# Attention scores packed into full banks, and one-hot tiles made by another engine

## The chip, the core and the metric

The kernel runs on one core of a Trainium2 chip. A core has five engines that run their own instruction streams and meet at semaphores: TensorE (PE in the profile; its weight loads are PEld), VectorE (DVE), ScalarE (ACT), GpSimd (POOL) and SyncE (SP), which here only issues DMAs. The metric is the time of one execution on the device in microseconds; several executions are timed and the median is taken.

## What is computed

Two layers, each an attention followed by a mixture of experts, on 8 batches of 512 tokens with 256 features. Cut to what matters here:

```python
x = x + tanh(g_xattn[0]) * L0_xattn(layernorm(x), ctx, ctx)   # 16 heads of 16, causal softmax
x = x + tanh(g_ffn[0])   * L0_ffn(layernorm(x))               # 32 experts, top 8, capacity 256
x = x + tanh(g_xattn[1]) * L1_xattn(layernorm(x), ctx, ctx)   # no causal mask
x = x + tanh(g_ffn[1])   * L1_ffn(layernorm(x))               # 8 experts, top 2
```

The first experts need, for each of their 32 * 256 = 8192 slots, the token that was routed there.

## The kernel before

Four phases run one after the other: `attention` for layer 0, `experts0`, `attention` for layer 1, `experts1`. The change lies in the first.

**The iterations.** `attention` works on one batch per iteration and has several batches in flight. Iteration `it` computes the scores of batch `cur = it`, the row maxima of batch `nxt = it + 1`, projections of later batches (`nn`, `n3`), and finishes earlier ones: `prev = it - 1` gets its output projection, second norm and routing, and `done = it - 2` gets its entries in the slot table. Iterations run from -3 to 9. Each is 64 steps `u`, and every engine's stream is written out by hand in the order of these steps; no scheduler changes it. An engine that has to wait holds back all that stands behind it in its stream.

**Scores, exponentials, values.** Heads come in four groups `g` of four. For a group, PE computes transposed scores, key tile `kt` (128 keys) against queries. With the causal mask only queries from `128 * kt` on are needed, so the four key tiles have 512, 384, 256 and 128 columns. `scores(b, u)` does one head and key tile per step: a matmul (L699), a second one (L702) that adds the mask to the diagonal 128 columns, into one of three PSUM banks `stb` of 512 columns. ACT's `exps` (L741) turns the bank into weights `pt`, which signals `st_free`. Then `values` (L713) multiplies the weights of one key tile of four heads by the values `va`, four matmuls into the four 32-row quarters of the bank `ob`. It is called once per key tile, at steps 6, 10, 14 and 18 after the group's start. After the fourth call ACT copies `ob` out (`outputs`, L746).

**Maxima.** The row maxima of `nxt` (PE L686 and L689, DVE L873 and L869) go through two banks `mxb`, at the steps 0, 2, 3, 5 and 7 of every eight.

**The other work of PE** stands in the table `TRIPS`: step, kind, batch. `x` at 24 and 31 transposes the normalised input of `n3`, `list` at 18, 20, 25 and 28 is the slot table, `p` the output projection, and so on. They share two banks `work`.

**The slot table.** For batch `done`, DVE makes four pairs of tiles (`one_hot`): `lo1` (128 tokens x 8 x 128, a one where the slot's low part is) and `hv` (x 8 x 64, the token's number where its high part is). DVE does so at 16 steps of the iteration, two instructions for `lo1` (L1021), one compare (L1024) and one multiplication (L1028) for `hv`. Each pair signals `lo_rdy` to the `list` matmuls (L665), and two pairs of buffers alternate. After the fourth `list`, DVE's `enlist` adds the result up (L1035 to L1039) at step 29 and frees the bank, which `x` at step 31 takes next.

**GpSimd** has little to do in this phase: the third parts of a three-way split of queries and keys (`rest` L1123, `low` L1129, at steps 61, 5, 16, 22) and the reciprocal roots of the two norms (`norm1` L1110 to L1117 at step 14, `norm2` L1134 to L1138 at step 29). ACT applies the first norm at steps 16, 17, 18 and 20 (L787, which signals `xn_rdy`), works on the split at 3 and 21 (L807), and applies the second norm at 33 to 36 (L798).

Of the kernel before, what the change touches and what calls it, by code (L numbers as in the profile page):

```python
# [248 lines left out]
def attention(c, layer, x_in, ctx_in, mask, wq, bq, wk, bk, wv, bv, wp, bp, wroute, x_out, rows,
# [17 lines left out]
    MAX_NO = {u: i for i, u in enumerate(sorted(MAX_BANKS))}  # L267

    with ExitStack() as ctx:
# [22 lines left out]
        pt = t_("pt", [P, 8, S])  # L292
# [292 lines left out]
        def _(pe):  # L585
# [119 lines left out]
            def values(b, g, kt):  # L705
                if g == 0 and kt == 0:
                    pe.wait_ge(evac["v"], 2 * b + 2)
                pe.wait_ge(s["st_free"], STEPS * b + 16 * g + 4 * kt + 4)
                if kt == 0:
                    wait(pe, s["ob_evac"], 4 * b + g)  # L710
                q0 = q_from(kt)
                for j in range(4):
                    last = pe.matmul(ob[32 * j:32 * j + 32, q0:S], va[b % 3][:, kt, 4 * g + j, :],  # L713
                                     pt[:, 4 * (kt % 2) + j, q0:S], start=kt == 0, stop=kt == NT - 1,
                                     tile_position=(0, 32 * j))
# [19 lines left out]
        def _(act):  # L735
            def exps(b, u):
                kt = u % 16 // 4
                if u % 4 == 0:
                    wait(act, s["pt_free"], 16 * b + u // 4 - 1)
                act.wait_ge(s["st_full"], STEPS * b + u + 1)  # L740
                act.activation(pt[:, u % 8, q_from(kt):S], stb[(STEPS * b + u) % N_ST][:, q_from(kt):S], ACT.Exp, scale=SCALE).then_inc(s["st_free"], 1)  # L741

            def outputs(b, g):
                act.wait_ge(s["pt_free"], 16 * b + 4 * g + 4)
# [892 lines left out]
```

## Time and profile before

| | us |
|---|---|
| median of three executions | 2114.45 (2112.62 to 2115.19) |
| the profiled execution, its own time | 2112.23 |
| its span, first to last instruction | 2110.4 |

The span divides into stages; the first `attention` takes the first five:

| us from the span's start | what runs |
|---|---|
| 0 to 120.4 | constants, weights, iterations -3 to -1 |
| 120.4 to 306.7 | iterations 0 to 2 (slot table from iteration 2 on) |
| 306.7 to 505 | iterations 3 to 5 (the first two of them full, with all kinds of work) |
| 505 to 608 | iterations 6 and 7, with no batch left to prepare |
| 608 to 655 | iterations 8 and 9: routing and slot table of the last two batches |
| 655 to 2110 | `experts0`, the second attention, `experts1` |

Reading the rows: a timeline row gives start, duration, engine, line, operation, output and inputs, the count of merged instructions, and in brackets the idle time before it with what ended it. A PE row's duration includes time in which the next matmul already runs, so PE's pace is read from the distance between starts.

### The profile page before, as it was taken

To read this page: it belongs to the slowest core of one execution; us is meant where nothing else is said; L and a number is where in the kernel's file an instruction comes from. 1 tells how busy PE (TensorE), PEld (TensorE's weight loads), DVE (VectorE), ACT (ScalarE), POOL (GpSimd) and SP (SyncE) were. 2 spreads that over 40 slices of the span, in tenths; PEclk is the share of its full clock that TensorE was granted. 3 is DMA by queue.
4 is the path that set the end of the run, shared out by engine and by line. 5 is a ranking of instruction groups with operands and counts; after the bars stand their busy time and mean duration, and the time that the engine had idled before them with its cause. 6 is when DMAs were issued, how large, how long until landed. Compare 5 with 4: busy or idle time off the path is not lost. (4 is left out here: it accounts for less than half of the span.)

```text
span 2110.4 us, 30079 instructions
## 1 busy us (share of the span) xinstructions
PE 1790.4 (85%) x10491; PEld 1054.6 (50%) x10491; DVE 1063.8 (50%) x2743; ACT 908.0 (43%) x1876; POOL 598.3 (28%) x577
## 2 busy tenths in 40 slices
PE   2789999999865999537899999999954999999995
PEld 1445555555534877413344444443331666666664
DVE  3446777887745444244867777778420211212121
ACT  1356766666541222113577777776730111111110
POOL 1312111210002778503211332221122233333322
PEclk9999999999986999858999999999976999999998
DMA  3444554434123788525323433331014133333314
GB/s 96 152 120 150 150 176 134 132 129 141 65 83 99 175 173 173 91 66 159 108 72 116 136 97 95 120 117 62 32 47 136 31 81 81 78 78 75 80 20 100
DMA packets 204245, 222.86 MB, mean 106 GB/s; under 512 B 33438, under 2 KB 195231, under 8 KB 203431
## 3 DMA queue, kind: packets, MB, share of 16 engines
q1 hardware_dynamic: 176458, 177.48, 27.4%
q0 software_dynamic: 27648, 43.60, 10.9%
q8 instruction: 78, 1.28, 0.3%
q14 instruction: 61, 0.50, 0.1%
HBM read 155.06 MB, written 86.93 MB: 115 GB/s over the span
## 5 line engine op out<-in xcount | busy, mean ns | idle before, releaser
L873 DVE TENSOR_REDUCE nmx<-mxb 128x1 f32<-128x512 f32 (+1 forms) x896 | 522.7, 609 | 282.5 <-PE mxb L686 146.6
L741 ACT ACTIVATE pt<-stb 128x512 f32<-128x512 f32 (+3 forms) x1024 | 501.0, 519 | 266.3 <-PE stb L702 140.8
L686 PE MATMUL mxb<-kst,qst 96*128 96x512 bf16 (+4 forms) x1024 | 332.3, 346 | 30.2 <-DVE nmx L873 21.3
L699 PE MATMUL stb<-qst,kst 99*128 99x512 bf16 (+4 forms) x1024 | 342.4, 345 | 14.8 <-DMA qst<-m3T 8.4
L713 PE MATMUL ob<-pt,va 128*32 128x512 f32 (+3 forms) x2048 | 233.7, 528 | 3.8 <-ACT oT L746 2.8
L1428 PE MATMUL e_h_bank<-e_xT,e_w 128*128 128x512 f32 x512 | 226.0, 600 | 6.1 <-ACT e_xT L1468 5.4
L699 PEld LDWEIGHTS stb<-qst,kst 102*128 102x128 bf16 (+1 forms) x1024 | 100.1, 99 | 258.1 <-ACT pt L741 167.3
L1442 PE MATMUL e_y_bank<-e_w,e_h 128*128 128x256 f32 x1024 | 226.9, 379 | 0.0
L1442 PEld LDWEIGHTS e_y_bank<-e_w,e_h 128*128 128x128 f32 x1024 | 192.9, 190 | 31.8 <-issue 7.2
L1123 POOL TENSOR_TENSOR qk<-qk,parts 128x512 f32<-128x512 f32 x64 | 72.8, 1160 | 432.8 <-ACT qk L774 225.7
L1582 POOL DMA_INDIRECT x_after_l<-e_y,e_token x64 | 99.6, 1556 | 281.7 <-DVE e_y L1547 267.0
L686 PEld LDWEIGHTS mxb<-kst,qst 99*128 99x128 bf16 (+1 forms) x1024 | 100.7, 99 | 133.9 <-DVE nmx L873 72.4
L1428 PEld LDWEIGHTS e_h_bank<-e_xT,e_w 128*128 128x128 f32 x512 | 97.8, 192 | 125.6 <-issue 125.0
L1477 ACT ACTIVATE e_h<-e_h_bank,e_b_e 128x512 f32<-128x512 f32 x64 | 44.0, 687 | 270.6 <-PE e_h_bank L1428 270.6
L1532 DVE TENSOR_SCALAR e_h<-e_h_bank,e_b_e 128x512 f32<-128x512 f32 x64 | 48.0, 750 | 171.5 <-PE e_h_bank L1428 171.5
L1543 DVE TENSOR_TENSOR e_y<-e_y_bank,e_b 128x512 f32<-128x512 f32 x32 | 22.1, 691 | 201.6 <-PE e_y_bank L1442 201.6
L1335 POOL DMA_INDIRECT x_after_l<-e_y,token x64 | 102.2, 1598 | 44.4 <-issue 17.6
L702 PE MATMUL stb<-hide_st,identb 128*128 128x128 bf16 x512 | 110.6, 221 | 0.0
L689 PE MATMUL mxb<-hide_max,identb 128*128 128x128 bf16 x512 | 110.0, 221 | 0.0
L1129 POOL TENSOR_TENSOR parts<-qk,parts 128x512 bf16<-128x512 f32 x64 | 73.9, 1175 | 97.8 <-ACT parts L807 97.8
L1144 POOL DMA_INDIRECT rows<-rowb,idx x64 | 63.9, 998 | 114.5 <-DVE idx L1000 97.4
L1243 PE MATMUL e_bank<-e_xT,e_guT 128*128 128x256 f32 x384 | 88.6, 380 | 1.0 <-DVE e_h L1299 1.0
(231 smaller groups left out, 2493.1 us busy)
## 6 DMA issues: line engine op xcount, KB each, us to landing
qk_parts<-parts SPq DMA_DIRECT2D x16, 1536.0 KB, 6.2
qst<-qk_parts SPq DMA_DIRECT2D x384, 64.0 KB, 2.3
kst<-qk_parts SPq DMA_DIRECT2D x384, 64.0 KB, 2.3
e_w<-in_L_ffn_w SPq DMA_DIRECT2D x16, 1024.0 KB, 7.4
rows<-rows SPq DMA_DIRECT2D x15, 1060.0 KB, 8.6
crow<-in_ctx SPq DMA_DIRECT2D x16, 512.0 KB, 3.9
x_after_l<-xres SPq DMA_DIRECT2D x16, 512.0 KB, 3.2
e_gu_nat<-in_L_ffn_gate_up_proj SPq DMA_DIRECT2D x64, 128.0 KB
```

Source lines behind the costliest of these rows:

```text
L686: last = pe.matmul(out, qst[par][0:rows_used, h, qt * P:(qt + 1) * P], kst[par][0:rows_used, h, 0:nk], start=True, stop=not causal)
L689: last = pe.matmul(out[:, nk - P:nk], c.identb[:, :], c.hide_max[:, :], start=False, stop=True)
L699: last = pe.matmul(out[:, q0:S], kst[par][0:ROWS, h, kt * P:(kt + 1) * P], qst[par][0:ROWS, h, q0:S], start=True, stop=not causal)
L702: last = pe.matmul(out[:, q0:q0 + P], c.identb[:, :], c.hide_st[:, :], start=False, stop=True)
L713: last = pe.matmul(ob[32 * j:32 * j + 32, q0:S], va[b % 3][:, kt, 4 * g + j, :], pt[:, 4 * (kt % 2) + j, q0:S], start=kt == 0, stop=kt == ...
L741: act.activation(pt[:, u % 8, q_from(kt):S], stb[(STEPS * b + u) % N_ST][:, q_from(kt):S], ACT.Exp, scale=SCALE).then_inc(s["st_free"], 1)
L873: last = dve.tensor_reduce(nmx[:, qt, h:h + 1], got[:, at:at + k_to(qt)], AX.X, ALU.max, negate=True)
L1243: last = pe.matmul(out, guT[par][:, ci, q, :], xT[par][:, ci, :], start=ci == 0, stop=ci == NC - 1)
L1335: pool.indirect_dma_start(x, bass.IndirectOffsetOnAxis(token[:, TILES * e + i:TILES * e + i + 1], 0), y[e % 3][:, i, :], None, bounds_chec ...
L1428: last = pe.matmul(hb[q % 4][:, :], w1_s[par][:, ci, k * P:(k + 1) * P], xT[par][:, ci, blk * HALF:(blk + 1) * HALF], start=ci == 0, stop= ...
L1442: last = pe.matmul(yb[t][:, i * D:(i + 1) * D], h[blk][:, k, (2 * t + i) * P:(2 * t + i + 1) * P], w2_s[par][:, k, :], start=k == 0, stop= ...
L1582: pool.indirect_dma_start(x, bass.IndirectOffsetOnAxis(token[par][:, i:i + 1], 0), y[par][:, i, :], None, bounds_check=T + SPARE - 1, oob_ ...
```

## The change

Scores of the first attention are packed so that every bank is full: a bank holds key tile 0 of one head, or tiles 3 and 1 of one head (128 + 384 columns), or tile 2 of two heads (256 + 256). A group has 10 banks in place of 16, at the steps 0, 2, 3, 5, 7, 8, 10, 11, 13, 15, and an exponential always takes 512 columns. `values` is called twice per group, at step 10 for key tile 0 and at step 18 for tiles 1, 3 and 2. The weights `pt` have 10 slots, one per bank of a group, in place of 8. For batches 0 to 6 GpSimd makes the one-hot tiles, 16 small instructions per pair, at the steps 6, 10, 13 and 19 of its stream; DVE makes those of batch 7 as before. There are three pairs of buffers. The second attention keeps one head and key tile per bank and four calls per group.

```diff
--- before.py
+++ after.py
@@ -226,6 +226,7 @@
+N_HOT = 3
...
+def score_banks(packed):
+    banks = {}
+    for g in range(GROUPS):
+        if not packed:
+            banks.update({16 * g + u: ((4 * g + u % 4, u // 4, 0),) for u in range(16)})
+            continue
+        for j, u in enumerate((0, 2, 3, 5)):
+            banks[16 * g + u] = ((4 * g + j, 0, 0),)
+        for j, u in enumerate((7, 8, 10, 11)):
+            banks[16 * g + u] = ((4 * g + j, 3, 0), (4 * g + j, 1, P))
+        for j, u in enumerate((13, 15)):
+            banks[16 * g + u] = ((4 * g + 2 * j, 2, 0), (4 * g + 2 * j + 1, 2, 2 * P))
     return banks
...
+    PACKED = causal
+    SCORE_BANKS = score_banks(PACKED)
+    N_SCORE = len(SCORE_BANKS)
+    SCORE_NO = {u: i for i, u in enumerate(sorted(SCORE_BANKS))}
+    VALUE_CALLS = {10: (0,), 18: (1, 3, 2)} if PACKED else {6: (0,), 10: (1,), 14: (2,), 18: (3,)}
+    N_CALL = len(VALUE_CALLS) * GROUPS
...
+    PT_SLOTS = 10 if PACKED else 8
...
-            lo1 = [t_(f"lo1_{i}", [P, 8, P], BF16) for i in range(2)]
-            hv = [t_(f"hv{i}", [P, 8, N_HI], BF16) for i in range(2)]
+            lo1 = [t_(f"lo1_{i}", [P, 8, P], BF16) for i in range(N_HOT)]
+            hv = [t_(f"hv{i}", [P, 8, N_HI], BF16) for i in range(N_HOT)]
...
-                wait(sp, s["st_full"], STEPS * (n - 2) + 16 * g + 16)
+                wait(sp, s["st_full"], N_SCORE * (n - 2) + N_SCORE // GROUPS * (g + 1))
...
             def scores(b, u):
...
-                wait(pe, s["st_free"], STEPS * b + u - N_ST + 1)
-                q0, h = q_from(kt), 4 * g + j
-                out = stb[(STEPS * b + u) % N_ST]
-                last = pe.matmul(out[:, q0:S], kst[par][0:ROWS, h, kt * P:(kt + 1) * P],
-                                 qst[par][0:ROWS, h, q0:S], start=True, stop=not causal)
-                if causal:
-                    last = pe.matmul(out[:, q0:q0 + P], c.identb[:, :], c.hide_st[:, :], start=False, stop=True)
+                if u not in SCORE_BANKS:
+                    return
+                no = N_SCORE * b + SCORE_NO[u]
+                wait(pe, s["st_free"], no - N_ST + 1)
+                bank = stb[no % N_ST]
+                for h, kt, at in SCORE_BANKS[u]:
+                    to = at if PACKED else q_from(kt)
+                    last = pe.matmul(bank[:, to:to + S - q_from(kt)], kst[par][0:ROWS, h, kt * P:(kt + 1) * P],
+                                     qst[par][0:ROWS, h, q_from(kt):S], start=True, stop=not causal)
+                    if causal:
+                        last = pe.matmul(bank[:, to:to + P], c.identb[:, :], c.hide_st[:, :], start=False, stop=True)
                 last.then_inc(s["st_full"], 1)
...
-                    if u == 2 and prev is not None:
-                        values(prev, 3, 3)
-                    if u % 4 == 2 and u > 2 and cur is not None:
-                        values(cur, (u - 6) // 16, (u - 6) % 16 // 4)
+                    for call, at in enumerate(sorted(VALUE_CALLS)):
+                        if u == at - 16 and prev is not None:
+                            values(prev, GROUPS - 1, call)
+                        if u >= at and (u - at) % 16 == 0 and cur is not None:
+                            values(cur, (u - at) // 16, call)
...
-                kt = u % 16 // 4
-                if u % 4 == 0:
-                    wait(act, s["pt_free"], 16 * b + u // 4 - 1)
-                act.wait_ge(s["st_full"], STEPS * b + u + 1)
-                act.activation(pt[:, u % 8, q_from(kt):S], stb[(STEPS * b + u) % N_ST][:, q_from(kt):S], ACT.Exp, scale=SCALE).then_inc(s["st_free"], 1)
...
+                if PACKED and u % 16 in (0, 7):
+                    wait(act, s["pt_free"], N_CALL * b + u // 16 * 2 - (1 if u % 16 == 0 else 0))
...
+                act.activation(pt[:, slot(b, u), q0:S], stb[no % N_ST][:, q0:S], ACT.Exp, scale=SCALE).then_inc(s["st_free"], 1)
...
+                    wait(dve, s["lo_rdy"], 4 * b)
...
-                        if u in ONE_HOT_AT:
+                        if u in ONE_HOT_AT and done == B - 1:
                             one_hot(done, ONE_HOT_AT.index(u) // 4, ONE_HOT_AT.index(u) % 4)
...
+            def one_hot(b, t):
+                pool.wait_ge(s["idx_rdy"], b + 1)
+                wait(pool, full["list"], 4 * b + t - N_HOT + 1)
+                for k in range(8):
+                    pool.tensor_scalar(lo1[t % N_HOT][:, k, :], c.lanes[:, :], lo_f[:, t, k:k + 1], None, ALU.is_equal)
+                for k in range(8):
+                    last = pool.tensor_scalar(hv[t % N_HOT][:, k, :], c.lanes[:, 0:N_HI], hi_f[:, t, k:k + 1], c.tok1[:, 0:1], ALU.is_equal, ALU.mult)
+                last.then_inc(s["lo_rdy"], 1)
...
+                    if layer == 0 and done is not None and done < B - 1 and u in (6, 10, 13, 19):
+                        one_hot(done, (6, 10, 13, 19).index(u))
```

PE, steps 18 and 19 of a full iteration, the start of a group's second half of `values`. Before, with the key tile 3 alone (L713) ahead of the first `list`:

```order
L686 MATMUL mxb_0<-kst_0,qst_0 128x512 [waits max_free_0]
L689 MATMUL mxb_0<-hide_max,identb 128x128
L713 MATMUL ob<-pt,va_0 32x128 [waits st_free_0]
L713 MATMUL ob<-pt,va_0 32x128 x3
L665 MATMUL work_0<-hv_0,lo_0_0 128x64 [waits lo_rdy_0,p_evac_0]
```

The same place after, where L757 is `values` and L703 `list`:

```order
L724 MATMUL mxb_0<-kst_0,qst_0 128x512 [waits max_free_0]
L727 MATMUL mxb_0<-hide_max,identb 128x128
L757 MATMUL ob<-pt,va_0 32x384 [waits st_free_0]
L757 MATMUL ob<-pt,va_0 32x384 x3
L757 MATMUL ob<-pt,va_0 32x128 x4
L757 MATMUL ob<-pt,va_0 32x256 x4
L703 MATMUL work_0<-hv_0,lo_0_0 128x64 [waits lo_rdy_0,p_evac_0]
```

Three key tiles now follow each other with one wait ahead of them.

GpSimd, one full iteration from `low` of the queries (step 5) to the second norm (step 29). Before:

```order
L1129 TENSOR_TENSOR parts<-qk,parts 128x512 x2
L1110 TENSOR_SCALAR rstd<-mv 128x4
L1112 TENSOR_TENSOR rstd<-rstd,mhalf 128x4
L1117 TENSOR_TENSOR shift_0<-minus_0,rstd 128x4
L1123 TENSOR_TENSOR qk<-qk,parts 128x512 x2
L1129 TENSOR_TENSOR parts<-qk,parts 128x512 x2
L1134 TENSOR_SCALAR rstdb<-mvb 128x4
```

After, with the same operations at L1181, L1162 to L1169, L1175 and L1186:

```order
L1181 TENSOR_TENSOR parts<-qk,parts 128x512 x2
L1203 TENSOR_SCALAR lo_0_0<-lanes,lo_f 128x128 x8
L1205 TENSOR_SCALAR hv_0<-lanes,hi_f,tok 128x64 x8
L1203 TENSOR_SCALAR lo_1_0<-lanes,lo_f 128x128 x8
L1205 TENSOR_SCALAR hv_0<-lanes,hi_f,tok 128x64 x8
L1203 TENSOR_SCALAR lo_2_0<-lanes,lo_f 128x128 x8
L1205 TENSOR_SCALAR hv_0<-lanes,hi_f,tok 128x64 x8
L1162 TENSOR_SCALAR rstd<-mv 128x4
L1164 TENSOR_TENSOR rstd<-rstd,mhalf 128x4
L1169 TENSOR_TENSOR shift_0<-minus_0,rstd 128x4
L1175 TENSOR_TENSOR qk<-qk,parts 128x512 x2
L1203 TENSOR_SCALAR lo_0_0<-lanes,lo_f 128x128 x8
```

Three tile pairs now stand ahead of the first norm and of the keys' `rest`, and the fourth ahead of the keys' `low`.

## Rows read from the trace of the kernel before

**Rows 1.** Busy time by stretch: length, busy time and count per engine, PE clock, DMA

```profile
306.70:505.00 198.30, 186.97 (x1659) 112.77 (x1658) 154.72 (x440) 127.77 (x298) 35.38 (x39) 1.00 0.45 139
...
608.00:655.00 47.00, 19.25 (x142) 14.52 (x142) 28.32 (x85) 5.37 (x10) 1.47 (x3) 0.61 0.14 48
```

**Rows 2.** Timeline of PE in the full iteration that starts at 306.7

```profile
313.30 0.22 PE L702 MATMUL stb<-hide_st,identb 128*128 128x128 bf16 x1
313.45 1.06 PE L713 MATMUL ob<-pt,va 128*32 128x512 f32 x8
314.45 0.34 PE L699 MATMUL stb<-qst,kst 102*128 102x384 bf16 x1
314.62 0.22 PE L702 MATMUL stb<-hide_st,identb 128*128 128x128 bf16 x1
314.68 0.38 PE L686 MATMUL mxb<-kst,qst 99*128 99x512 bf16 x1
...
326.04 0.22 PE L689 MATMUL mxb<-hide_max,identb 128*128 128x128 bf16 x1
326.19 0.43 PE L713 MATMUL ob<-pt,va 128*32 128x128 f32 x8
326.54 0.41 PE L665 MATMUL work<-hv,lo 128*128 128x64 bf16 x8
```

**Rows 3.** PE's waits in iterations 2 to 4: us in total, times, longest

```profile
PE work L665 <- DVE hv L1028: 4.0, 3, 1.3
PE work L607 <- DVE listed L1036: 3.3, 3, 1.2
```

**Rows 4.** PE's waits for DVE's maxima in iteration 6

```profile
PE mxb L686 <- DVE nmx L873: 2.1, 4, 1.1
```

**Rows 5.** PE's waits for ACT in iteration 0, then in iteration 7

```profile
PE stb L699 <- ACT pt L741: 1.2, 3, 0.6
...
PE stb L699 <- ACT pt L741: 3.0, 3, 2.2
```

**Rows 6.** Groups of GpSimd by form, whole span: busy us, mean ns, idle before

```profile
L1123 POOL TENSOR_TENSOR qk<-qk,parts 128x512 f32<-128x512 f32 x64 | 72.8, 1160 | 432.8 <-ACT qk L774 225.7 <-ACT qk L778 207.0
...
L1110 POOL TENSOR_SCALAR rstd<-mv 128x4 f32<-128x4 f32 x16 | 3.8, 234 | 162.4 <-DVE minus L861 162.4
...
L196 POOL TENSOR_SCALAR_AFFINE_SELECT identb<-identb 128x128 bf16<-128x128 bf16 x1 | 0.3, 293 | 0.0
...
L190 POOL MEMSET identb<- 128x128 bf16 x1 | 0.2, 218 | 0.0
```

**Rows 7.** Timeline of GpSimd in the same full iteration

```profile
311.66 2.58 POOL L1129 TENSOR_TENSOR parts<-qk,parts 128x512 bf16<-128x512 f32 x2 [2.91 <-ACT parts L807]
322.94 0.25 POOL L1110 TENSOR_SCALAR rstd<-mv 128x4 f32<-128x4 f32 x1 [8.70 <-DVE minus L861]
...
331.39 2.28 POOL L1129 TENSOR_TENSOR parts<-qk,parts 128x512 bf16<-128x512 f32 x2 [4.57 <-ACT parts L807]
```

**Rows 8.** Timeline of ACT, same iteration: first norm applied, first and last part

```profile
324.65 0.59 ACT L787 ACTIVATE xn<-xin,shift,rstd 128x256 f32<-128x256 f32 x1
...
329.30 0.59 ACT L787 ACTIVATE xn<-xin,shift,rstd 128x256 f32<-128x256 f32 x1
```

**Rows 9.** Timeline of PE, same iteration: first `x` and fourth `list`

```profile
332.81 0.60 PE L607 MATMUL work<-ident,xn 128*128 128x128 f32 x4
...
337.64 0.41 PE L665 MATMUL work<-hv,lo 128*128 128x64 bf16 x8 [1.32 <-DVE hv L1028]
```

**Rows 10.** Groups of ACT by form in the same full iteration

```profile
L741 ACT ACTIVATE pt<-stb 128x512 f32<-128x512 f32 x16 | 9.2, 595 | 3.0 <-PE stb L702 3.0
...
L741 ACT ACTIVATE pt<-stb 128x128 f32<-128x128 f32 x18 | 4.5, 282 | 6.4 <-PE stb L702 6.3
```

**Rows 11.** A group of DVE by form in the same full iteration

```profile
L1021 DVE TENSOR_TENSOR lo<-lanes,lo_f 128x512 bf16<-128x512 bf16 x8 | 5.8, 733 | 0.0
```

**Rows 12.** Timeline of PE in iteration 8: the fourth `list`

```profile
625.36 0.61 PE L665 MATMUL work<-hv,lo 128*128 128x64 bf16 x8 [3.12 <-DVE hv L1028]
```

More of the change, by code:

```diff
@@ L245, in shared_banks @@
         banks[u + 7] = ((h + 1, 3, 0),)
+    return banks
+def score_banks(packed):
[10 more added lines that the diff above has]
+            banks[16 * g + u] = ((4 * g + 2 * j, 2, 0), (4 * g + 2 * j + 1, 2, 2 * P))
     return banks
@@ L291, in attention @@
         va = [t_(f"va{i}", [P, NT, HEADS, 32]) for i in range(3)]
-        pt = t_("pt", [P, 8, S])
+        pt = t_("pt", [P, PT_SLOTS, S])
         oT = [t_(f"oT{i}", [P, S]) for i in range(2)]
@@ L496, in k_to, with quad, slot, weights_of @@
             return (qt + 1) * P if causal else S
+        def quad(b, u):
+            return (STEPS * b + u) // 4
+        def slot(b, u):
+            if PACKED:
+                return SCORE_NO[u] % (N_SCORE // GROUPS)
+            return quad(b, u) % (PT_SLOTS // 4) * 4 + u % 4
+        def weights_of(b, g, kt, j):
+            if not PACKED:
+                return pt[:, slot(b, 16 * g + 4 * kt + j), q_from(kt):S]
+            at, first = {0: (0, j), 1: (P, 4 + j), 2: (2 * P * (j % 2), 8 + j // 2), 3: (0, 4 + j)}[kt]
+            return pt[:, first, at:at + S - q_from(kt)]
         @block.sync
@@ L664, in trip @@
                     for k in range(8):
-                        done = pe.matmul(out[:, N_HI * part:N_HI * (part + 1)], lo1[part % 2][:, k, :], hv[part % 2][:, k, :],
+                        done = pe.matmul(out[:, N_HI * part:N_HI * (part + 1)], lo1[part % N_HOT][:, k, :], hv[part % N_HOT][:, k, :],
                                          start=k == 0, stop=k == 7)
@@ L703, in scores, with values @@
                 last.then_inc(s["st_full"], 1)
-            def values(b, g, kt):
-                if g == 0 and kt == 0:
+            def values(b, g, call):
+                at = sorted(VALUE_CALLS)[call]
+                if g == 0 and call == 0:
                     pe.wait_ge(evac["v"], 2 * b + 2)
-                pe.wait_ge(s["st_free"], STEPS * b + 16 * g + 4 * kt + 4)
-                if kt == 0:
+                scored = sum(u < 16 * (g + 1) and u // 16 == g and {kt for _, kt, _ in SCORE_BANKS[u]} <= USED[at] for u in SCORE_BANKS)
+                pe.wait_ge(s["st_free"], N_SCORE * b + N_SCORE // GROUPS * g + scored)
+                if call == 0:
@@ L710, in values @@
                     wait(pe, s["ob_evac"], 4 * b + g)
[L711 to L715, printed above, removed]
+                for kt in VALUE_CALLS[at]:
+                    for j in range(4):
+                        last = pe.matmul(ob[32 * j:32 * j + 32, q_from(kt):S], va[b % 3][:, kt, 4 * g + j, :],
+                                         weights_of(b, g, kt, j), start=kt == 0, stop=kt == VALUE_CALLS[max(VALUE_CALLS)][-1],
+                                         tile_position=(0, 32 * j))
@@ L736, in exps @@
             def exps(b, u):
[L737 to L741 removed]
+                if u not in SCORE_BANKS:
+                    return
+                no = N_SCORE * b + SCORE_NO[u]
+                if PACKED and u % 16 in (0, 7):
+                    wait(act, s["pt_free"], N_CALL * b + u // 16 * 2 - (1 if u % 16 == 0 else 0))
+                if not PACKED and u % 4 == 0:
+                    last = quad(b, u) - PT_SLOTS // 4
+                    wait(act, s["pt_free"], last // (4 // len(VALUE_CALLS)) + 1)
+                act.wait_ge(s["st_full"], no + 1)
+                q0 = 0 if PACKED else q_from(SCORE_BANKS[u][0][1])
+                act.activation(pt[:, slot(b, u), q0:S], stb[no % N_ST][:, q0:S], ACT.Exp, scale=SCALE).then_inc(s["st_free"], 1)
             def outputs(b, g):
[L744 removed]
+                act.wait_ge(s["pt_free"], N_CALL * b + len(VALUE_CALLS) * (g + 1))
                 wait(act, full["o"], 4 * b + g - 1)
```

15 lines of the change are left out of this document (8 added, 7 removed).

## The prediction

> **What bounds the kernel now.** I read the stretches first [rows 1]. In iterations 3 to 5 PE is busy 187.0 of 198.3 us; DVE has 154.7, ACT 127.8, GpSimd 35.4. So the first attention goes at PE's pace, and work that leaves DVE or ACT counts only where PE waits for it. A PE that is busy in this sense could still stand behind late starts, so next I read the distance between its starts [rows 2]: 512 columns of `values` take 1.00 us, 384 columns of scores 0.17, a mask 0.06. These repeat to the hundredth, so PE runs full, at the granted clock of 1.00 (2.4 GHz), except where a wait shows. In the full iterations 2 to 4 the waits are two: the fourth `list` waits for DVE's one-hot tile, 1.32 us each time, and `x` at step 31 waits for `enlist`, 1.1 on average [rows 3]. In the thinner iteration 6 PE also waits 2.1 us for maxima of a DVE that has fallen behind [rows 4]; in iteration 7 it waits 3.0 us for ACT, and 1.2 in iteration 0 [rows 5]. In 608 to 655 nothing bounds but the chain of one batch's steps; PE is busy 19.3 of 47 us at a clock of 0.61 [rows 1].
>
> **The change part by part.**
>
> *Values in two calls.* A mask is followed by the next bf16 matmul after 0.06 us, but by `values` after 0.15: 0.09 for the turn to the four-quarter form. And the call with 128 columns takes 0.35, with 512 columns 1.00 [rows 2]; a straight line through them gives 0.217 per 128 columns and a rest of 0.13 that doesn't grow with the columns. Merging three calls into one saves two turns per group: 2 x 4 groups x 8 batches = 64. Each saves 0.09 if blocks inside a call still pay the rest, 0.22 if they don't: 5.8 to 14.1 us. All of it is on PE's path. I take the middle, 0.16 x 64 = **10 us**.
> The Trainium skill, TensorEngine Tiling (Array Packing), Key Properties, says that changing the tiling mode drains the engine while changing the tile alone doesn't. The 0.09 agrees; if the rest of 0.13 is the drain as well, the saving is the 14.1, and the sum below would be 4 us lower.
>
> *Exponentials.* 64 become 40 per batch, with the same columns: 16 x (0.595 + 0.282) plus the middle sizes become 40 x 0.595 = 23.8 us [rows 10]; a 512 costs far less than four times a 128. ACT isn't the bound, so this gives only PE's waits for ACT back. Three banks now hold about 4.8 steps of work in place of 3, so iteration 0's waits go: **1 us** of 1.2 [rows 5].
>
> *Scores.* The same 64 + 64 matmuls per batch with the same columns: nothing. They now come only at steps that also carry maxima, so PE reaches the next maxima sooner at some steps and later at others. In the full iterations no wait for maxima is among PE's long ones, and where DVE was loaded with tiles and PE had less to do it came to 2.1 us [rows 4]. I take 0, and up to that 2.1 per batch as the other end.
>
> *One-hot tiles off DVE.* DVE loses the 5.8 us of L1021 per iteration [rows 11] and the two smaller groups that make `hv`. *They land on GpSimd*, which has no row for such an instruction. Below, a 128-column AFFINE_SELECT, one input and one output of just this shape, takes 0.29 us; a memset 0.22. A TENSOR_SCALAR of 4 columns takes 0.23, and the slope of a two-input TENSOR_TENSOR, (1.160 - 0.23) / 508, is 1.83 ns per column [rows 6]. So a 128-column one costs 0.25 to 0.46 and a 64-column one 0.15 to 0.34, a pair of tiles (8 of each) 3.2 to 6.4 us. Nearest is the AFFINE_SELECT, with a little for the scalar read per partition: 0.32 and 0.24, **4.5 us per pair**. That is 18 us per iteration on an engine that is mostly idle, but in a fixed order.
>
> What stands behind it: `low` ends at 314.24, +7.5 after the iteration's start at 306.7 [rows 7]; with `values` now 1.7 us long at step 2, ACT gets to its part later, so +8.4. Three pairs follow. Then `norm1`, which now starts at 322.94 after 8.7 us of idle, +16.2 [rows 7]. Then ACT's four norm instructions with two exponentials and a copy between them; they now run from 324.65 to 329.89 [rows 8], and without waits for PE would take about 3.6. `x` on PE at step 24 needs them. So `x` can start at 8.4 + 3t + 1.6 + 3.6 = 13.6 + 3t, where t is the time per pair; PE comes to it at +26.1 now [rows 9], +25.5 after. At t = 3.9 PE begins to wait; at 4.5 it waits 1.6 us. The fourth pair comes after `norm1` and `rest` (3.7 with the start at 8.4): ready at 12.1 + 4t, against +29.0 for the fourth `list` (now 337.64 less the wait of 1.32 and the merged calls [rows 9]). At 4.5 that is +30.1, covered by the wait at `x`. So in iterations 2 to 4 a wait of 1.6 replaces one of 1.32: **+1 us** in all, where t = 3.2 gives -4 and t = 6.4 gives +17 (7.3 against 1.32). The wait for `enlist` stays almost whole: after the fourth `list` DVE must take the maxima of step 29 and then add up, with `x` two steps behind. I leave 0.9 of the 1.1: **-0.5** for the three.
> GpSimd's `low` of the keys, now at 331.39, shifts by about 2.7 us at t = 4.5, and SP's store of the parts with it; the stacked rows it feeds are needed an iteration later, so this is hidden.
>
> *Thin iterations.* 5 has no `norm1`, so the fourth pair is ready at 10.5 + 4t = +28.5: a tile wait like those of rows 3 goes, 1.3, and I add as much for DVE's lag behind it: **-2.5**. 6 has no split on GpSimd; the tile wait of 1.3 and the 2.1 of maxima go [rows 3, 4]: **-3.5**. In 7, 3.0 us of waits for ACT [rows 5] come from the second norm, which stands behind `enlist`; the tiles end at 1 + 4t = +19 of about +20: **-2.5**.
>
> *Tail.* In iteration 8 the fourth `list` runs at 625.36 [rows 12]. On GpSimd the four pairs start near 608 and end near 626: **+1**, and the last call of `values` is 1.3 longer with nothing beside it, partly paid back in iteration 7: **+1**. At t = 3.2 this is -1, at 6.4 +9.
>
> *Sum.* -10 - 1 + 1 - 0.5 - 2.5 - 3.5 - 2.5 + 2 = **-17**. The profiled execution took 2112.2, so 2095; the median of the runs stands 2.2 above it, so a median of runs may come out up to 2 higher. I say **2096**.
>
> **Rivals.**
> *GpSimd is dear (slower).* If a compare costs what the two-input rows say, t = 6.4: iterations 2 to 4 lose 17, iteration 5 loses 6 (10.5 + 4t is then 36 against 29, less the 1.3), 7 loses 5, the tail 9, against 10 of calls, 2 in iteration 6 and 1.5 of the rest: +23, 2137 with the median's 2. It decides from t = 5.4, where losses and gains are even; at t = 6 it is about 2130. For it: no row shows the operation, and a scalar per partition is an extra operand. Against: AFFINE_SELECT's 0.29.
> The Trainium skill, GPSIMD Engine Reference, Engine selection, speaks against the change: elementwise work belongs on VectorE, though it calls one-input work roughly line-rate, which would be this forecast's side. No row here settles it.
> *GpSimd is cheap and merged blocks flow.* t = 3.2 and 14.1 us of calls: -14 - 1 - 4 - 1 - 3 - 4 - 4 - 1 = -32, 2080.
> *The gains are given back (no change).* Bursts of banks make PE wait for DVE's maxima, 2.1 us per batch as in rows 4, in 8 batches: -17 + 17, so 2112 to 2114. For it: banks and maxima now share their steps. Against: DVE has at least 5.8 us less to do per iteration [rows 11].
>
> **How the numbers follow.** Forecast 0.50 (2084 to 2108), cheap 0.20, given back 0.14, dear 0.16. Two of ten outside means cutting the lower half of the cheap case and the upper half of the dear one: 2076 to 2120. About 0.2%, 4 us, is what can be told from no change: faster 0.72, same 0.12, slower 0.16.
>
> **What would show it.** Right: GpSimd rows of 128 columns near 0.32 us and of 64 near 0.24; two turns fewer per group, with the long call near 1.6 us between starts; no PE wait for DVE's `hv`, but one of 1 to 2 us at `x` of step 24 put down to ACT's `xn`, behind GpSimd; the `listed` wait still there; iteration 6 at least 3.5 us shorter. Wrong: compare rows over 0.4 us, `list` waiting for GpSimd, ACT idle behind `norm1`, or full iterations that stay at 66 us with waits for maxima.

## The result, and the profile after

The changed kernel takes 2228.74 us (median of 2227.05 to 2235.4) against 2114.82 for the kernel before in the same comparison: a ratio of 1.0543, 95% interval 1.0527 to 1.0559. It is slower by 114 us; the forecast was 2096, and the range ended at 2120. The profiled execution took 2227.05 us, with a span of 2225.3.

First the operation that no row of before showed. Groups of GpSimd by line: operation, output and input, count, then busy us and mean ns.

```profile
L1203 POOL TENSOR_SCALAR lo<-lanes,lo_f 128x128 bf16<-128x128 bf16 x224 | 131.1, 630 | 74.0 <-DVE hi_f L1062 74.0
L1205 POOL TENSOR_SCALAR hv<-lanes,hi_f,tok 128x64 bf16<-128x64 bf16 x224 | 126.0, 616 | 0.0
```

The forecast took 0.32 and 0.24 us; they are 0.63 and 0.62. The records overlap a little: from start to start, in the rows below, it is 0.58 and 0.55, and eight of each make 9.1. Next GpSimd's timeline in the full iteration 3, which answers to [rows 7]: start, duration, what ran; in brackets the idle time ahead.

```profile
321.79 2.32 POOL L1175 TENSOR_TENSOR qk<-qk,parts 128x512 f32<-128x512 f32 x2 [30.52 <-ACT qk L829]
328.89 2.27 POOL L1181 TENSOR_TENSOR parts<-qk,parts 128x512 bf16<-128x512 f32 x2 [4.78 <-ACT parts L858]
331.14 4.67 POOL L1203 TENSOR_SCALAR lo<-lanes,lo_f 128x128 bf16<-128x128 bf16 x8
335.80 4.48 POOL L1205 TENSOR_SCALAR hv<-lanes,hi_f,tok 128x64 bf16<-128x64 bf16 x8
...
358.34 0.30 POOL L1162 TENSOR_SCALAR rstd<-mv 128x4 f32<-128x4 f32 x1
...
362.24 4.68 POOL L1203 TENSOR_SCALAR lo<-lanes,lo_f 128x128 bf16<-128x128 bf16 x8
366.90 4.48 POOL L1205 TENSOR_SCALAR hv<-lanes,hi_f,tok 128x64 bf16<-128x64 bf16 x8
371.32 2.29 POOL L1181 TENSOR_TENSOR parts<-qk,parts 128x512 bf16<-128x512 f32 x2
```

From 331.14 to 371.32 GpSimd has no idle time. A pair follows the last after 9.1 us (331.14 to 340.23), and `norm1` starts at 358.34, 36.6 us after GpSimd's first row of the iteration, where it had come 16.2 into the iteration [rows 7]. Who waits for this is in PE's waits, 120 to 780 us (total, times, longest):

```profile
PE work L703 <- POOL hv L1205: 75.4, 18, 8.5
PE stb L741 <- ACT pt L792: 27.7, 4, 10.2
PE work L703 <- DVE hv L1080: 10.2, 4, 5.6
```

The third row belongs to batch 7, whose tiles DVE still makes; `listed` is left with 1.2 us. The second row is ACT behind the late `norm1`: its norm instructions stand ahead of exponentials in its stream, and PE then finds no free `stb` bank. The prediction had put this wait at `x` of step 24; PE meets it earlier, at the scores. In order of time, those of PE's rows from 340 to 377 us (iteration 3) that have a wait:

```profile
349.42 0.61 PE L703 MATMUL work<-hv,lo 128*128 128x64 bf16 x8 [3.41 <-POOL hv L1205]
...
361.70 0.29 PE L741 MATMUL stb<-qst,kst 102*128 102x128 bf16 x1 [8.76 <-ACT pt L792]
...
371.43 0.41 PE L703 MATMUL work<-hv,lo 128*128 128x64 bf16 x8 [2.65 <-POOL hv L1205]
...
374.03 1.11 PE L645 MATMUL work<-ident,xn 128*128 128x128 f32 x4 [0.89 <-DVE listed L1088]
```

These four give 15.7 us, and the iteration is 20.3 longer. The rest shows in the whole iteration 3, after and then before: length, busy time and count of PE, PEld, DVE, ACT and POOL, PE's clock, DMA.

```profile
323.06:409.92 86.86, 68.14 (x557) 42.50 (x555) 44.64 (x132) 41.16 (x79) 48.34 (x79) 0.88 0.41 124
306.53:373.05 66.52, 63.11 (x556) 38.10 (x554) 51.77 (x148) 43.78 (x103) 12.34 (x15) 1.00 0.48 148
```

All of PE's waits in it are 18.9 us against 3.4, so 15.5 more, and PE is busy 5.0 us longer with as many matmuls: between and after long waits its granted clock falls. PE by stretches of 20 us: length, busy time and count, clock, DMA:

```profile
320.00:340.00 20.00, 18.07 (x147) 1.00 0.67 196
340.00:360.00 20.00, 9.54 (x80) 0.81 0.00 1
360.00:380.00 20.00, 14.75 (x100) 0.67 0.33 105
380.00:400.00 20.00, 19.20 (x189) 1.00 0.51 148
```

Before, the mean over iterations 3 to 5 was 1.00, 2.4 GHz [rows 1]; 0.67 and 0.81 are means between that and 1.2 GHz. In the stretch of 0.81 PE waits 3.4 us for GpSimd and most of the 8.8 for ACT behind it.

DVE's cast of the slot numbers runs once per iteration, at its start (L1009 before, L1061 after); counted from it, this is where the fourth `list` stands and how long the iteration is:

| iteration | fourth `list`, before | after | later by | length before | after | longer by |
|---|---|---|---|---|---|---|
| 2 | 31.1 | 48.4 | 17.3 | 66.2 | 84.8 | 18.7 |
| 3 | 31.1 | 48.4 | 17.3 | 66.5 | 86.9 | 20.3 |
| 4 | 31.1 | 48.4 | 17.3 | 66.5 | 86.6 | 20.1 |
| 5 | 30.9 | 46.8 | 15.8 | 64.2 | 82.1 | 17.9 |
| 6 | 26.6 | 36.8 | 10.2 | 59.0 | 68.6 | 9.5 |
| 7 | 19.9 | 36.8 | 16.9 | 44.5 | 58.8 | 14.3 |
| 8 | 18.2 | 36.8 | 18.6 | 37.3 | 56.0 | 18.6 |
| sum | | | 113.4 | | | 119.4 |

Outside these iterations the span is 4.5 us shorter, 2.1 of it ahead of iteration 2. So the loss goes with the lateness of the fourth `list`, to about 3 us in each iteration, and nothing of the packing's gain shows but a little in iterations without tiles.

### The profile page after: what moved, and what is told of

It is laid out like the page before. It is cut to its first block and busy times, and to the rows that moved or that the text cites. A ratio compares the mean times of both kernels' runs of the same rounds, so it can differ in the third digit from the quotient of the medians.

```text
span 2225.3 us, 30165 instructions
## 1 busy us (share of the span) xinstructions
PE 1805.7 (81%) x10491; PEld 1076.4 (48%) x10491; DVE 1010.3 (45%) x2631; ACT 886.9 (40%) x1684; POOL 851.0 (38%) x1025
## 5 line engine op out<-in xcount | busy, mean ns | idle before, releaser
L792 ACT ACTIVATE pt<-stb 128x512 f32<-128x512 f32 x832 | 475.1, 598 | 323.8 <-PE stb L744 199.9
L724 PE MATMUL mxb<-kst,qst 96*128 96x512 bf16 (+4 forms) x1024 | 340.5, 354 | 34.4 <-DVE nmx L924 25.0
L741 PE MATMUL stb<-qst,kst 99*128 99x512 bf16 (+4 forms) x1024 | 336.9, 354 | 37.4 <-ACT pt L792 29.7
L1175 POOL TENSOR_TENSOR qk<-qk,parts 128x512 f32<-128x512 f32 x64 | 73.0, 1165 | 426.4 <-ACT qk L825 223.3
L757 PE MATMUL ob<-pt,va 128*32 128x512 f32 (+3 forms) x2048 | 224.2, 533 | 2.7 <-ACT pt L792 1.7
L1203 POOL TENSOR_SCALAR lo<-lanes,lo_f 128x128 bf16<-128x128 bf16 x224 | 131.1, 630 | 74.0 <-DVE hi_f L1062 74.0
L1205 POOL TENSOR_SCALAR hv<-lanes,hi_f,tok 128x64 bf16<-128x64 bf16 x224 | 126.0, 616 | 0.0
L744 PE MATMUL stb<-hide_st,identb 128*128 128x128 bf16 x512 | 115.6, 232 | 0.0
```

The lines of the kernel that those rows point to most:

```text
L724: last = pe.matmul(out, qst[par][0:rows_used, h, qt * P:(qt + 1) * P], kst[par][0:rows_used, h, 0:nk], start=True, stop=not causal)
L741: last = pe.matmul(bank[:, to:to + S - q_from(kt)], kst[par][0:ROWS, h, kt * P:(kt + 1) * P], qst[par][0:ROWS, h, q_from(kt):S], start=Tru ...
L744: last = pe.matmul(bank[:, to:to + P], c.identb[:, :], c.hide_st[:, :], start=False, stop=True)
L757: last = pe.matmul(ob[32 * j:32 * j + 32, q_from(kt):S], va[b % 3][:, kt, 4 * g + j, :], weights_of(b, g, kt, j), start=kt == 0, stop=kt = ...
L792: act.activation(pt[:, slot(b, u), q0:S], stb[no % N_ST][:, q0:S], ACT.Exp, scale=SCALE).then_inc(s["st_free"], 1)
L1203: pool.tensor_scalar(lo1[t % N_HOT][:, k, :], c.lanes[:, :], lo_f[:, t, k:k + 1], None, ALU.is_equal)
```

## The experiments

**Packing alone.** All tiles back on DVE; the third pair of buffers stays:

```diff
-                        if u in ONE_HOT_AT and done == B - 1:
+                        if u in ONE_HOT_AT:
```

> Packed scores and two calls of values as in the changed kernel, with all one-hot tiles left on DVE. Theory 1 (GpSimd's tiles cost about 9.1 us a pair and all that stands behind them, packing itself gains): 2100 to 2107 us, 8 to 15 below the 2115 of before, with the 64 merged calls worth 6 to 14. Rival (packing itself costs time, because banks and maxima share their steps): above 2117, with PE waits for DVE's maxima of over 2 us per batch.

Measured: 2119.52, ratio 1.0023 (1.0012 to 1.0034). Packing is slower by itself: the rival's time, though its waits for maxima are 1.2 us and not over 2. PE's waits in iteration 3, against 1.3 for `hv`, 1.2 for `listed`, 0.7 for DVE's sequencer (DVEq) and 0.2 for `m3T` before. `nmx` are the row maxima, `xres` the residual sum, `listed` the slot table's sum; `onT` and `m3T` are copies that ACT makes of a PE result for a later matmul:

```profile
PE work L645 <- DVE listed L1088: 1.6, 1, 1.6
PE mxb L724 <- DVE nmx L924: 1.2, 1, 1.2
PE work L645 <- DVE xres L957: 1.0, 1, 1.0
PE work L703 <- DVE hv L1080: 0.8, 1, 0.8
PE work L676 <- ACT onT L810: 0.7, 1, 0.7
PE work L665 <- ACT m3T L864: 0.6, 1, 0.6
```

With two smaller ones these are 6.4 us against 3.4, and the iteration is 68.2 long against 66.5: the work between waits shrank by about 1.4 us (PE is busy 61.7 against 63.1), and the new waits took 3.0. The merged call itself does what it should:

```profile
326.44 1.50 PE L757 MATMUL ob<-pt,va 128*32 128x384 f32 x24
327.87 0.41 PE L703 MATMUL work<-hv,lo 128*128 128x64 bf16 x8
```

The three tiles have 768 columns, 1.30 us at the 0.217 per 128 of the prediction; the block takes 1.43. So the rest of 0.13 is paid once per call.

**Tiles on GpSimd alone.** The scores unpacked:

```diff
-    PACKED = causal
+    PACKED = False
```

> One-hot tiles on GpSimd as in the changed kernel, scores and values unpacked as before. Theory 1: 2230 to 2245 us, since the whole loss comes from GpSimd and packing only gave some of it back. Rival (packing costs a large part of the 114): 2140 to 2200.

Measured: 2219.48, ratio 1.0499 (1.0484 to 1.0515), below the first theory's range and above the rival's. The tiles account for 105 of the 114 us, and packing comes on top with 9 (2228.7 against 2219.5), where it was to take 11 away. In iteration 3 (82.1 us long, against 86.9 with packing) PE waits 16.9 us, 15.3 of them at once for ACT behind `norm1`, and is busy 65.2. So of the 4.8 that packing adds there, 2.0 are more waits and 2.9 a longer busy PE, whose mean clock is 0.88 against 0.90.

**Half the tiles.** GpSimd makes `lo`, DVE makes `hv` (scores packed):

```diff
-                for k in range(8):
-                    last = pool.tensor_scalar(hv[t % N_HOT][:, k, :], c.lanes[:, 0:N_HI], hi_f[:, t, k:k + 1], c.tok1[:, 0:1], ALU.is_equal, ALU.mult)
```

> As the changed kernel, but GpSimd makes only the lo1 tiles (8 instructions, about 4.7 us a pair) and DVE the hv tiles. This gives the chain on GpSimd nearly the 4.5 us per pair that the prediction assumed. If only the size of that term was wrong and the rest of the sum holds: 2095 to 2106 us, with a wait of 1 to 3 us at x of step 24 and none for GpSimd's tiles in the full iterations. Rival (other terms fail too, for example because a waiting PE loses its clock, or because two engines must finish each pair): 2110 to 2150.

Measured: 2113.93, ratio 0.9998 (0.9988 to 1.0008). Eight `lo` instructions took 4.96 us here, near the 4.5 that the forecast had put on a whole pair, and the loss is gone. But nothing is gained: the time lies in the rival's range and not in the 2095 to 2106 of a sum in which only this size was wrong, so other terms failed too. In the full iterations PE waits for ACT, 4.1 us in six waits, none over 1.2, and once 0.3 for `lo`. In iteration 3 the two for ACT are 1.4, and 0.2 more for `xn`: the 1.6 behind `norm1` that the prediction worked out for such a dose. The waits that packing alone makes for `nmx`, `onT` and `m3T` stand beside them, a full iteration takes 68.1 to 69.1 us, and in the thinner ones PE waits 9.2 for `lo`. So the chain on GpSimd behaves as worked out once its price is put in; what packing was to gain is missing here as well.

**The forms.** In the constants of the kernel before, GpSimd runs four instructions of each of nine forms:

```diff
+                pool.tensor_scalar(bdst[:, 0 + k, :], bsrc[:, 0:P], scal[:, k:k + 1], None, ALU.is_equal)
+                pool.tensor_scalar(bdst[:, 4 + k, :], bsrc[:, 0:P], 1.0, None, ALU.is_equal)
+                pool.tensor_scalar(bdst[:, 8 + k, 0:4], bsrc[:, 0:4], scal[:, k:k + 1], None, ALU.is_equal)
+                pool.tensor_scalar(bwide[:, 512 * k:512 * k + 512], bsrc[:, :], scal[:, k:k + 1], None, ALU.is_equal)
...
+                pool.tensor_scalar(fdst[:, 20 + k, :], fsrc[:, 0:P], scal[:, k:k + 1], None, ALU.mult)
...
+                pool.tensor_scalar(bdst[:, 28 + k, 0:64], bsrc[:, 0:64], scal[:, k:k + 1], scal[:, 0:1], ALU.is_equal, ALU.mult)
+                pool.tensor_scalar(bdst[:, 32 + k, 0:64], bsrc[:, 0:64], scal[:, k:k + 1], None, ALU.is_equal)
```

> The kernel before with nine groups of four TENSOR_SCALAR instructions of GpSimd added to the constants, to price the form (in order: compare bf16 128 columns with a scalar per partition; the same with a constant; 4 columns with a scalar per partition; 512 columns; f32 compare 128; f32 multiply 128; bf16 multiply 128; compare and multiply bf16 64 columns; compare bf16 64). Theory A (the scalar per partition costs a fixed 0.4 us): constant form under 0.35 us, 4 columns at 0.45 or more, 512 columns about 0.9. Theory B (the compare is slow per column): 4 columns near 0.25, 512 columns near 1.6, multiply near 0.35. Theory C (bf16 is slow): the f32 forms near 0.35.

```profile
L221 POOL TENSOR_SCALAR bwide<-bsrc,scal 128x512 bf16<-128x512 bf16 x4 | 6.2, 1566 | 0.0
...
L215 POOL TENSOR_SCALAR bdst<-bsrc,scal 128x128 bf16<-128x128 bf16 x4 | 2.4, 610 | 0.1
L225 POOL TENSOR_SCALAR fdst<-fsrc,scal 128x128 f32<-128x128 f32 x4 | 2.4, 605 | 0.0
...
L229 POOL TENSOR_SCALAR bdst<-bsrc,scal 128x64 bf16<-128x64 bf16 x4 | 2.2, 576 | 0.0
L217 POOL TENSOR_SCALAR bdst<-bsrc 128x128 bf16<-128x128 bf16 x4 | 2.0, 526 | 0.1
L231 POOL TENSOR_SCALAR bdst<-bsrc,scal 128x64 bf16<-128x64 bf16 x4 | 1.7, 438 | 0.0
L219 POOL TENSOR_SCALAR bdst<-bsrc,scal 128x4 bf16<-128x4 bf16 x4 | 1.1, 294 | 0.0
```

From 4 to 512 columns the slope is (1566 - 294) / 508 = 2.5 ns per column. Type and operation change nothing (bf16 compare 610, fp32 multiplication 605), a constant in place of the scalar per partition saves 84 ns, and the second operation of `hv` costs 138 on 64 columns. None of the theories holds whole. What was missed is plain: one input, but a steeper slope than two. The prediction's 1.83 joined a TENSOR_SCALAR to a TENSOR_TENSOR [rows 6]; from TENSOR_TENSOR's own rows before, 4 columns in 0.20 us (L1117) and 512 in 1.16, it is 1.89. Of `hv`'s price the second operation is 0.14, for which the forecast had nothing.

**A dose below the slack.** Scores as before the change; of four pairs GpSimd makes the last alone, in the third pair of buffers, `lo` ahead of its own `low` and `hv` behind it:

```diff
-                        if u in ONE_HOT_AT and done == B - 1:
+                        if u in ONE_HOT_AT and (done == B - 1 or ONE_HOT_AT.index(u) < 12):
...
-                    if layer == 0 and done is not None and done < B - 1 and u in (6, 10, 13, 19):
+                    if layer == 0 and done is not None and done < B - 1 and u in (4, 6):
```

> The kernel before in its scores, exponentials and calls of values; of the four tile pairs of a batch GpSimd makes only the last (its lo part ahead of its own low of the queries, its hv part behind it), DVE the other three. Theory 'a dose below the slack': two times 4.6 us per iteration end about 7 us before the fourth list needs them, and norm1 starts at most 1 us later; DVE loses a quarter of its tile work, so the 1.3 us wait for DVE's hv in iterations 2 to 4 goes and the lag in 5 to 7 shrinks: 2104 to 2110. Rival 'GpSimd slows DVE': DVE's two-input compares of the other pairs take 0.2 us longer each while GpSimd works, as the hv compare did with the lo tiles on GpSimd (0.99 against 0.81 us), and little is left: 2111 to 2116. Rival 'slow tiles cost something anywhere': a quarter of the loss of after, some 2135.

Measured: 2102.27, ratio 0.9932 (0.9918 to 0.9946). The first theory holds, a little beyond its range. PE's wait for `hv` in iterations 2 to 4 [rows 3] is gone and that for `listed` shrinks to 0.7 at most; a full iteration takes 64.4 us against 66.5. GpSimd pays for working beside DVE's tiles:

```profile
L1209 POOL TENSOR_SCALAR lo<-lanes,lo_f 128x128 bf16<-128x128 bf16 x48 | 36.0, 765 | 55.6 <-DVE hi_f L1066 55.6
L1213 POOL TENSOR_SCALAR hv<-lanes,hi_f,tok 128x64 bf16<-128x64 bf16 x48 | 31.7, 676 | 0.0
```

**The same with packed scores.** The previous experiment's edits on the changed kernel.

> As e5_one_pair, with the packed scores and the two calls of values of the changed kernel. Theory 'packing alone falls behind DVE': the new waits of the packed kernel with all tiles on DVE (8.9 us per full iteration against 6.2) are for a DVE that is late, so a quarter of the tile work less takes back about 2 us per iteration: 2104 to 2112, as fast as e5_one_pair or faster. Rival 'the waits are the bursts of banks and maxima themselves': the waits stay, 2114 to 2120, slower than e5_one_pair by the 4 us that packing alone cost.

Measured: 2107.12, ratio 0.9957 (0.9944 to 0.9971). It lies in the range of the first theory, but that also claimed it would not be slower than the run before, and it is, by 4.9 us, near the 3.8 that packing cost in the first experiment. PE's waits in iterations 2 to 4 are still 1.2 each time for `nmx`, 1.0 for `xres`, 0.7 for `onT` and 0.6 for `m3T`. (The expectation's 8.9 and 6.2 us per iteration are 6.4 and 3.4 by PE's own rows above.) So a DVE that is late with tiles is not their cause; in the changed kernel, where DVE makes none, iteration 3 still has 1.2 for `nmx`, 0.7 for `onT` and 0.7 for `m3T`.

**Three calls.** Packed, tiles on DVE, key tiles 1 and 3 at step 14 and tile 2 at 18:

```diff
-    VALUE_CALLS = {10: (0,), 18: (1, 3, 2)} if PACKED
+    VALUE_CALLS = {10: (0,), 14: (1, 3), 18: (2,)} if PACKED
```

> Packed scores, all tiles on DVE, but values in three calls per group: key tile 0 at step 10, 1 and 3 at step 14, 2 at step 18. Against the packed kernel with two calls (2119.5) this gives one turn per group back, 32 in all, at 0.1 to 0.2 us each: 3 to 6 us of PE's work. Theory 'the block of 1.7 us makes the new waits': shorter blocks take the waits for maxima and for ACT away, 2 us and more per iteration, and the time is 2106 to 2115. Rival 'the full banks at steps shared with the maxima make them': waits stay and the time is 2121 to 2126.

Measured: 2122.92, ratio 1.0041 (1.0026 to 1.0057), the rival's time. But its waits are not the rival's. In iterations 2 to 4:

```profile
PE work L645 <- DVE xres L957: 3.1, 3, 1.0
PE work L665 <- ACT m3T L864: 2.9, 3, 1.0
PE work L696 <- DVEq L1014: 2.8, 3, 1.0
PE work L703 <- DVE hv L1080: 2.6, 3, 0.9
PE mxb L724 <- DVE nmx L924: 1.2, 4, 0.3
```

`onT` is gone, `nmx` fell from 1.2 to 0.3, and `listed` from 4.4 us to 0.9 in all; `xres` stayed, `m3T` grew from 0.6 to 1.0 and DVE's sequencer from 0.1 to 0.9. A full iteration is 67.2 us long, 1.0 shorter than with two calls. That this doesn't reach the total lies behind iteration 4: iterations 5 and 6 are 3.4 and 3.0 longer, and from 440 to 509 us the clock was 0.93, where the packed kernel had 1.00 from 443 to 509. What made it fall there is open.

Which waits went gave the next theory. Each of them stands behind a step from which a call of `values` had gone. `xres` is one: the bank for `x` at step 24 comes free after DVE has added the last `p` of step 21. The kernel before had a call there, at step 22:

```profile
330.37 0.27 PE L640 MATMUL work<-bp,onesb 128*128 128x256 bf16 x1
...
330.79 1.06 PE L713 MATMUL ob<-pt,va 128*32 128x512 f32 x8
331.79 0.34 PE L699 MATMUL stb<-qst,kst 102*128 102x384 bf16 x1
```

From `p` (330.37) to `x` (332.81 [rows 9]) PE had 2.44 us of work, 1.00 of it this call, and no wait. With packing alone it has about 1.4 (to 332.94, 0.06 after the start of the mask), then waits:

```profile
331.53 0.27 PE L678 MATMUL work<-bp,onesb 128*128 128x256 bf16 x1
...
332.88 0.22 PE L727 MATMUL mxb<-hide_max,identb 128*128 128x128 bf16 x1
334.14 0.66 PE L645 MATMUL work<-ident,xn 128*128 128x128 f32 x4 [1.05 <-DVE xres L957]
```

`onT` at step 15 had the call of step 14 ahead of it, `m3T` at 39 that of 38, `listed` at 31 that of 30, `nmx` at 2 that of 62. The three calls put one back at 14, 30, 46 and 62 and none at 22 or 38, with the banks where they were: just the waits behind 14, 30 and 62 shrank.

**Cover put back.** Packed, tiles on DVE, two calls as before, but at the steps 6 and 14 of a group, where calls stood before the change:

```diff
-        for j, u in enumerate((0, 2, 3, 5)):
+        for j, u in enumerate((0, 1, 2, 3)):
...
-        for j, u in enumerate((7, 8, 10, 11)):
+        for j, u in enumerate((5, 6, 7, 8)):
...
-        for j, u in enumerate((13, 15)):
+        for j, u in enumerate((10, 11)):
...
-    VALUE_CALLS = {10: (0,), 18: (1, 3, 2)} if PACKED
+    VALUE_CALLS = {6: (0,), 14: (1, 3, 2)} if PACKED
```

> Packed scores and all tiles on DVE as in e1_pack_only, with the same number of calls and turns, but the banks stand at the steps 0 to 3, 5 to 8, 10 and 11 of a group and the two calls of values at 6 and 14, where the kernel before had its calls for key tiles 0 and 2. Theory 'the calls were cover': in the packed kernel PE waits 1.05 us for xres at step 24, 0.69 for onT at step 15, 0.65 for m3T at step 39 and 1.2 for nmx at step 2, each right behind a step (22, 14, 38, 62) from which a call of 0.6 to 1.0 us had gone; with calls there again these waits shrink to below 0.3 each, 2 to 3 us per iteration, and the saved turns show: 2103 to 2110. Rival 'full banks that share steps with maxima, or a DVE that is too loaded, make the waits': 2115 to 2122, as e1_pack_only.

Measured: 2105.92, ratio 0.9962 (0.9948 to 0.9976). The theory holds. PE's waits in iterations 2 to 4, all that the view lists:

```profile
PE work L703 <- DVE hv L1080: 4.3, 3, 1.4
PE work L696 <- DVEq L1014: 4.0, 3, 1.3
PE work L645 <- DVE listed L1088: 1.8, 3, 0.7
PE ob L757 <- ACT oT L797: 0.5, 3, 0.2
PE mxb L724 <- DVE nmx L924: 0.5, 3, 0.2
```

`xres`, `onT` and `m3T` are gone and `nmx` is at 0.2; the waits for `hv` and for DVE's sequencer grew, and in all a full iteration has 3.8 us of waits against 6.4. It takes 64.9 us against 68.2. The edit moved the banks as well as the calls; that the calls did it rests on which waits went, here and in the run with three calls, where the banks stood still. Not all of the gain is that: the profiled runs differ by 15.8 us, 9.9 of them in iterations 2 to 4, 2.6 ahead of them and 3.9 behind iteration 8, where the edit changes nothing.

**Both repairs.** The cover, and the last pair on GpSimd.

> e9_cover with the last tile pair of each batch on GpSimd as in e5_one_pair and e6_one_pair_packed. Theory 'the calls were cover': packing's own gain of about 1 us per batch now adds to the 13.5 us of e5_one_pair: 2090 to 2098, faster than e5_one_pair. Rival: as e6_one_pair_packed, 2105 to 2110.

Measured: 2096.77, ratio 0.9919 (0.9903 to 0.9935), the fastest of all, inside the theory's range. The full iteration takes 63.05 us. The gains add only in part: 9.4 and 13.5 give 18.6 together. In a full iteration they nearly add, 1.7 and 2.1 against 3.5; iteration 5 takes 64.2 us, where the pair on GpSimd alone took 62.4. Why it gives less there no run shows.

**The order on GpSimd.** The changed kernel, with `norm1` and the keys' `rest` behind the first pair, ahead of the other three:

```diff
-                    if layer == 0 and done is not None and done < B - 1 and u in (6, 10, 13, 19):
-                        one_hot(done, (6, 10, 13, 19).index(u))
+                    if layer == 0 and done is not None and done < B - 1 and u in (6, 15, 17, 19):
+                        one_hot(done, (6, 15, 17, 19).index(u))
```

> The changed kernel with another order on GpSimd: after the first pair come norm1 and the keys' rest, then the pairs two to four, then the keys' low. Theory 'the end of the fourth pair sets the iteration': it ends about 49.5 us after the iteration's start as before, PE stands at list in place of ACT's norm, and the time stays at 2222 to 2232. Rival 'what stands behind the tiles in GpSimd's order costs for itself': the waits of 8.5 to 10.2 us for an ACT that stands behind norm1 go in iterations 2 to 4 and nothing takes their place: 2198 to 2206.

Measured: 2230.53, ratio 1.0547 (1.0527 to 1.0566). ACT's wait is gone, and it gives nothing, as the first theory said: PE stands at `list` for what it had stood at the scores. From 238 to 612 us that wait is

```profile
PE work L703 <- POOL hv L1205: 63.8, 14, 7.9
```

against 37.0 in 11 waits in the changed kernel, whose 27.7 for ACT went over into it almost whole. In both orders the end of the fourth pair sets the iteration.

## Why the prediction was wrong

*The step that failed* is the price of a tile pair under "One-hot tiles off DVE": 4.5 us forecast, 9.1 measured. The bounds were 0.25 to 0.46 us for 128 columns and 0.15 to 0.34 for 64; both rows lie above their upper ends, t is 9.1 against 3.2 to 6.4, and the value taken, "nearest is the AFFINE_SELECT", was half of it. The AFFINE_SELECT of 128 columns still takes 0.29 us in the changed kernel, beside TENSOR_SCALARs of 0.63; why they differ no run shows. The one TENSOR_SCALAR row that there was, 4 columns in 0.23 us [rows 6], gave a fixed part and no slope, and the slope of the two-input rows wasn't an upper bound for it. Where a form is absent, another operation's slope bounds nothing; the range should have stayed open upward, or asked from which t the sign turns (5.4, it said so itself) and how well 5.4 was excluded. It wasn't.

The Trainium skill, GPSIMD Engine Reference, Engine selection, which the prediction weighed, advises against elementwise work here, and the result agrees; its remark that one-input work goes at roughly line rate isn't borne out by 2.5 ns per column against the 1.89 of two inputs. No step above rests on this sentence.

*The formulas around the price held.* With t = 9.1 the fourth pair is ready at 12.1 + 4t = 48.5; its `list` stands at 48.4 by the table, 49.6 after GpSimd's first row of the iteration. In iteration 5 it is 10.5 + 4t = 46.9 against 46.8, in 7 1 + 4t = 37.4 against 36.8, and the same 36.8 in 6 and 8. `x` of step 24 was to start at 13.6 + 3t = 40.9 and starts at 41.1, without a wait of its own, since PE had stood at the scores. So "GpSimd is dear" was the right rival, at 0.16; its 2137 was the same price error at the other end. It also has a slip: at t = 6.4 the fourth pair (12.1 + 4t, 8.7 past 29.0) binds and not `x` (7.3), so by the prediction's own formulas iterations 2 to 4 lose 22 there and not 17.

*Values in two calls.* A saving of 0.16 per turn was taken between 0.09 and 0.22. The block of 1.43 us puts it at the upper end: three calls of 256, 128 and 384 columns at 0.217 per 128 and 0.13 each, with a turn of 0.09 each, are 1.96; the merged one is 1.52; 0.22 per turn. PE's busy time in a full iteration agrees only roughly: for eight turns it fell by 1.4 with packing alone and by 2.1 with the cover, 0.18 and 0.26 each. "All of it is on PE's path" failed twice: with tiles on GpSimd PE waits anyway, and with tiles on DVE the calls' places mattered, since they covered DVE's and ACT's latencies. The prediction named the work that hides other edits, but not what the moved calls had hidden.

*Gains given back.* This rival held for packing alone, with the wrong place: maxima were 1.2 us of 6.4 us of waits. *Exponentials*: ACT was no bound, and iteration 0's waits for it, 1.2, went, as said. *`enlist`*: 0.9 was to stay in each of iterations 2 to 4; two waits of 1.2 in all did. *Thin iterations and tail*: the gains of 2.5, 3.5 and 2.5 became losses of 17.9, 9.5 and 14.3 and the tail's +2 one of 18.6; with the tiles alone they are 17.4, 8.3, 15.0 and 18.5, so it is the price.

What stays open: packing costs 4 alone and 9 on top of the tiles. In iteration 3 its new waits and PE's busy time at a lower clock account for the difference (2.0 and 2.9 us, above); why the clock costs more with packing no run shows. It may be that the waits come in three places there and in one without it, with work at the low clock between them.

## What to carry to other kernels

Before work goes to an idle engine, find its price in a row of the same operation, or run the one instruction; until then, work out the price at which the sign turns, and don't take a neighbouring operation for a bound. Move a dose that fits into the slack of the engine's own chain, not all of it: one pair of four gained 13.5 us where four lost 105. And when calls are merged, ask which waits the moved ones had covered, and leave a call where it covers one.

## What the chip showed that was not expected

TENSOR_SCALAR on GpSimd goes at 2.5 ns per column with one input, TENSOR_TENSOR with two at 1.89, and AFFINE_SELECT took 0.29 us for the 128 columns that cost a TENSOR_SCALAR 0.61.

GpSimd and DVE slow each other, but not where the expectation of "A dose below the slack" had it. On GpSimd 128 columns took 630 ns where DVE made no tiles and 765 where DVE made three of the four pairs beside it. DVE's compare is hardly slowed by the tiles. With `lo` on GpSimd the four `hv` compares of an iteration had a mean of 1.0 us, but two of them ran beside `lo` and took 0.75 and 0.67; the other two, 1.13 and 1.49, began beside `low` and `rest`, GpSimd's instructions with two inputs. One of each, from iteration 3:

```profile
322.05 0.75 DVE L1081 TENSOR_TENSOR hv<-lanes,hi_f 128x512 bf16<-128x512 bf16 x1
...
333.18 1.49 DVE L1081 TENSOR_TENSOR hv<-lanes,hi_f 128x512 bf16<-128x512 bf16 x1
```

The kernel before has the same: 1.21 for the compare that begins beside `low`, 0.67 to 0.68 for the other three. The Trainium skill, GPSIMD Engine Reference, Specifications, has the two engines share their interfaces to SBUF and contend when DVE's instruction reads two inputs from it; DVE's compares are of that form, and these numbers agree.

TensorE's granted clock fell to 0.81 and 0.67 in two stretches of 20 us in which it waited for GpSimd, or for ACT behind it, and was back at 1.00 in the next 20 us.
